# Moving a small transfer from SyncE's queue to GpSimd's, and a large store and its subtractions earlier on GpSimd

## The reference, cut to what matters

```python
x = x + jnp.tanh(g_xattn[0]) * _L0_xattn_ref(_layernorm(x, axis=-1), ctx_2048, ctx_2048)
x = x + jnp.tanh(g_ffn[0]) * _L0_ffn_ref(_layernorm(x, axis=-1), L0_ffn_wg, L0_ffn_W, L0_ffn_b)
# attention, x is (16, 128, 512): 8 heads of 16 features, 512 x 512 scores for each head
qk = jnp.einsum('bdm,bdn->bmn', qh, kh) * scale
sm = jax.nn.softmax(qk, axis=-1)
ret = jnp.einsum('bmn,bcn->bcm', sm, vh)
# feed-forward: each of 2048 tokens goes to the one of 8 experts with the largest logit
```

## Time and profile before

| | |
|---|---|
| median of 3 runs | 585.63 us (582.6 to 586.23) |
| the profiled execution: its time | 586.23 us |
| the profiled execution: its span | 584.6 us, from the first to the last instruction |
| busy shares of the span | PE 88%, DVE 72%, ACT 60%, POOL 60% |
| mean granted TensorE clock | 0.977 |

### The profile page before, as it was taken

One profiled execution on the slowest core, in us unless ns is written; L12 is line 12 of the kernel. 1 busy time (PEld: TensorE's weight loads), 2 busy tenths in 40 slices (PEclk: granted clock), 3 DMA queues, 4 the chain that ended last, 5 costly groups with the idle time before them and its releaser, 6 DMA issues. The chain is left out here.

```text
span 584.6 us, 9983 instructions
## 1 busy us (share of the span) xinstructions
PE 515.4 (88%) x2603; PEld 183.0 (31%) x2603; DVE 422.7 (72%) x831; ACT 349.7 (60%) x429; POOL 352.5 (60%) x568
## 2 busy tenths in 40 slices
PE   0389999889887999998999999998979979899994
PEld 0012323222323232323333232323322235355551
DVE  5898988768785789888999998989998565112121
ACT  3217887758684778786887877886855842111110
POOL 7444478756564657685767777885473446544532
PEclk9999999989997899999999999999997999999998
DMA  4875457666666486776557555545540154643410
GB/s 141 237 154 178 140 174 201 217 176 185 185 191 176 131 229 197 197 205 175 161 162 213 166 171 153 165 127 158 127 116 24 38 181 163 186 138 98 127 55 0
DMA packets 50392, 90.90 MB, mean 156 GB/s; under 512 B 22018, under 2 KB 24066, under 8 KB 50320
## 3 DMA queue, kind: packets, MB, share of 16 engines
q1 hardware_dynamic: 36096, 65.28, 40.9%
q0 software_dynamic: 10560, 24.93, 12.9%
q10 hardware_dynamic: 3696, 0.23, 0.4%
HBM read 66.91 MB, written 28.41 MB: 163 GB/s over the span
## 5 line engine op out<-in xcount | busy, mean ns | idle before, releaser
L948 DVE TENSOR_REDUCE neg_max<-ps_ring 128x1 f32<-128x512 f32 x480 | 309.0, 682 | 48.9 <-PE ps_ring L1315 47.6
L852 ACT ACTIVATE probs<-ps_scores 128x1024 f32<-128x1024 f32 x256 | 250.1, 1022 | 75.0 <-PE ps_scores L1334 74.2
L1315 PE MATMUL ps_ring<-stacks 96*128 96x512 bf16 x480 | 171.2, 393 | 14.8 <-DVE neg_max L948 13.7
L1334 PE MATMUL ps_scores<-stacks 128*128 128x512 bf16 x512 | 157.1, 390 | 14.9 <-DMA stacks<-shift_parts 8.5
L1357 PE MATMUL ps_pv<-probs,v_ones 128*32 128x512 f32 x992 | 135.2, 618 | 0.0
L1315 PEld LDWEIGHTS ps_ring<-stacks 96*128 96x128 bf16 x480 | 47.1, 98 | 171.4 <-DVE neg_max L948 125.1
L1420 PE MATMUL ps_scores<-w_sb,f_xt 128*128 x184 | 83.2, 593 | 0.0
L1334 PEld LDWEIGHTS ps_scores<-stacks 128*128 128x128 bf16 x512 | 48.2, 102 | 70.4 <-ACT probs L852 21.6
L836 ACT COPY f_xt<-ps_scores 128x512 f32<-128x512 f32 x23 | 13.5, 586 | 72.2 <-PE ps_scores L1401 72.2
L605 POOL CAST shift_parts<-shift 16x128 bf16<-16x128 f32 x32 | 9.0, 282 | 64.6 <-DVE shift L955 64.3
L1420 PEld LDWEIGHTS ps_scores<-w_sb,f_xt 128*128 128x128 f32 x184 | 34.5, 190 | 33.0 <-issue 32.2
(11 more groups left out here) (149 smaller groups left out, 499.8 us busy)
## 6 DMA issues: line engine op xcount, KB each, us to landing
stacks<-parts_dram SPq DMA_DIRECT2D x224, 64.0 KB, 3.0
parts_dram<-prep POOLq DMA_DIRECT2D x15, 768.0 KB, 5.4
w_sb<-w_t SPq DMA_DIRECT2D x16, 512.0 KB, 4.9
recs_dram<-rec SPq DMA_DIRECT2D x16, 512.0 KB, 3.2
stacks<-parts_dram SPq DMA_DIRECT2D x32, 192.0 KB, 3.4
prep<-x_perm SPq DMA_DIRECT2D x16, 256.0 KB, 2.9
prep<-k_perm SPq DMA_DIRECT2D x16, 256.0 KB, 3.2
v_in<-v_t SPq DMA_DIRECT2D x16, 256.0 KB, 3.3
```

The lines of the kernel that those rows point to most:

```text
L852: nc.scalar.activation(probs[:, k % 2, 2 * jp:2 * jp + 2], ps_scores[:, jp], ACT.Exp).then_inc(exp_done, 1)
L948: nc.vector.tensor_reduce(neg_max[:, g, j, c:c + 1], ps_ring[:, SLOT[tile]], AX.X, ALU.max, negate=True).then_inc(ring_free, 1)
L1315: nc.tensor.matmul(ps_ring[:, SLOT[tile]], q_stack[0:KS, into.p, g, j, c * 128:(c + 1) * 128], k_stack[0:KS, into.p, g, j], start=True, st ...
L1334: last = nc.tensor.matmul(ps_scores[:, jp, j % 2], k_stack[0:KA, B.p, g, j, c * 128:(c + 1) * 128], q_stack[0:KA, B.p, g, j], start=True, ...
```

## The change

The changed kernel does the following, and nothing else:

- SyncE has no `load_shift` any more. GpSimd issues group 0's three transfers too, and does so behind `rstd2(B-1)`, just before `copy_values(B+1)`; the one for batch 0 goes between `split_maxima(Batch(0, 0), 0)` and `rstd1(Batch(1, 0))`.
- On GpSimd `lows(B+3)`, with its 768 KB store, stands directly behind `rests(B+3)`, ahead of `add_high(B-1)`; it was behind `rstd2(B-1)`.
- On VectorE `invert_taken(B-1, 1)` goes from behind tile (2, 0) to behind (2, 2), `stats2(B-1)` from (5, 2) to (6, 0), `mean2(B-1)` from (5, 3) to (6, 1).

```diff
--- before.py
+++ after.py
@@ -405,15 +405,6 @@
                     at = 32 * j + g * DH
                     sp.dma_start(scale[at:at + DH, g], recip_dram[g, j].partition_broadcast(DH)).then_inc(recips_in[g], 16)
 
-            def load_shift(B, g):
-
-                sp.wait_ge(shift_ready, B.b * 2 + (g + 1))
-                if not isinstance(B.b, int):
-                    stand_alone(sp)
-                for t in range(NP):
-                    sp.dma_start(q_stack[KS + t:KS + t + 1, B.p, g].rearrange("o j (c m) -> o (j c) m", c=NC),
-                                 shift_parts[:, g, t]).then_inc(shift_in[g], 16)
-
             def load_weights(B):
 
                 n = NC * NE * DM // NB
@@ -449,8 +440,6 @@
             for g in range(NG):
                 load_stack(Batch(0, 1), g)
             load_values(Batch(0, 1))
-            sp.wait_ge(pads_in, 16)
-            load_shift(Batch(0, 0), 0)
             load_rows_keys(Batch(1, 1))
 
             def emit(B, prev, prev2, nxt, prep):
@@ -467,8 +456,6 @@
                     sp.wait_ge(dve_const, DVE_CONSTS)
                 if stack:
                     load_stack(B.plus(2), 0)
-                if not B.known(NB - 1):
-                    load_shift(B.plus(1), 0)
                 if not isinstance(B.b, int) or B.b + 4 < NB:
                     load_rows_keys(B.plus(4))
                 if by_transfer(B):
@@ -708,6 +695,7 @@
             rests(Batch(0, 1))
             lows(Batch(0, 1))
             split_maxima(Batch(0, 0), 0)
+            load_shift(Batch(0, 0), 0)
             rstd1(Batch(1, 0))
             rests(Batch(1, 0))
             lows(Batch(1, 0))
@@ -738,6 +726,7 @@
                     add_low(B.plus(-1))
                 if prep:
                     rests(B.plus(3))
+                    lows(B.plus(3))
                 if B.known(RANKED[1]):
                     number_places(1)
                     store_tokens(*GROUPS[1])
@@ -746,8 +735,7 @@
                 split_maxima(B.plus(1), 0)
                 if prev:
                     rstd2(B.plus(-1))
-                if prep:
-                    lows(B.plus(3))
+                load_shift(B.plus(1), 0)
                 copy_values(B.plus(1))
                 if B.known(RANKED[0]):
                     pool.wait_ge(table_set, 16)
@@ -1236,11 +1224,11 @@
                             mean1(B.plus(3))
                         if prev:
                             attended = B.plus(-1)
-                            if at == (2, 0):
+                            if at == (2, 2):
                                 invert_taken(attended, 1)
-                            if at == (5, 2):
+                            if at == (6, 0):
                                 stats2(attended)
-                            if at == (5, 3):
+                            if at == (6, 1):
                                 mean2(attended)
                         if by_transfer(B):
                             if at == (6, 2):
```

## The result

The changed kernel takes **608.21 us** (median of 4, 604.59 to 614.85) against 585.93 of the kernel before beside it: a ratio of 1.037, 95% interval 1.029 to 1.045. It is slower by 22 us; forecast were 11. One of the four executions (614.85) was in a slower state with a lower clock, and the ratio leaves it out. The profiled execution took 612.86 us, with a span of 611.2 (before: 586.2 and 584.6): some 4 us of the 26.6 between the two are this execution's own.

The account below looks back on a forecast made before the run. Batches 2 to 5 were taken as bound by SyncE's queue, 6 to 14 by PE. 586.2 + 8.7 for GpSimd's chain + 3 for the earlier store gave 597.9 profiled, 597 us as median; range 586 to 610.

Parts of the forecast that it names:

- rival C: Rival: early store delays the sums, batches 1 to 7 pass 29 us, shift lands 0.5 later afterwards; 611 us; chance 0.12.
- GpSimd's chain in batch 8: GpSimd's order summed from batch start: three shift issues begin at 22.8 us, landing at 26.4, where PE could start at 24.3.
- Batches 8 to 14: Attention stage's second half, held by the shift's landing: batch 8 +2.1 us, batches 9 to 13 +6.7, batch 14 +1.0.
- Batches 0 and 15 have one half of the chain or none: 0: First and last attention batches: GpSimd's longer order was taken to add nothing, 0 us.
- The batches of the first half: Batches 1 to 7: -1.1 us by the sum over GpSimd's order and +3 for the early store, +1.9 forecast.
- The congestion term: Batches 1 to 7: the earlier store competes with SyncE's loads and delays the sums; +3 us, bounds 0 to 10.
- C's mark: Sign of the congestion rival: VectorE's wait for the sums grows over 10 us in all.
- C's other half: Batches 8 to 14: the shift's own landing is 0.5 us longer, +3.5 in all.
- The landing in the loop: Batch 4's sum: issues start at 24.0 us, last one 1.0 later, 2.6 more to landing, giving 27.6.
- A: Rival: SyncE's relief brings batches 2 to 7 to about 26.5 us; needs first issue by 21.0; 576 us; chance 0.08.
- B's mechanism: Rival, even: the shift lands in 1.5 us instead of 2.6, each of 14 batches 1.1 shorter; 582 to 591; chance 0.22.
- The signs: Expected in the changed profile: longer PE shift waits, alike batches, no GpSimd idle before `add_high`, issues near 22.8, SyncE's loads earlier.

Follow-up runs that it names:

- e8_first: The changed kernel with batch 0's shift issued by SyncE again, with a semaphore of its own: 604.41 us, ratio 1.032 to the kernel before.
- e11_both: The changed kernel with group 0's shift directly behind `split_maxima`, ahead of `rstd2`, and batch 0's shift back on SyncE: 593.43 us, ratio 1.014 to the kernel before.
- e5_after_early: The changed kernel with group 0's shift moved directly behind `split_maxima`, ahead of `rstd2`: 596.55 us, ratio 1.019 to the kernel before.
- e7_fill: The changed kernel with eight extra matmuls on TensorE at each batch's start, ahead of the wait for the shift: 600.07 us, ratio 1.029 to the kernel before.
- e3_lows: The kernel before with only `lows` and its store moved ahead of `add_high`: 589.79 us, ratio 1.010.
- e10_sp: The change without its queue move: `lows` early and VectorE's new places, shift left on SyncE: 583.44 us, ratio 0.996 to the kernel before.
- e6_store: The changed kernel with the 768 KB store moved behind the shift's transfers, `lows`' subtractions staying early: 601.50 us, ratio 1.026 to the kernel before.
- e1_early: The kernel before with only group 0's shift moved to GpSimd, directly behind `split_maxima`, ahead of `rstd2`: 579.91 us, ratio 0.993.
- e2_late: The kernel before with only group 0's shift moved to GpSimd, behind `rstd2` with `lows` behind it: 593.34 us, ratio 1.016.

## Why the prediction was right, and where its size was off

The direction, the late shift behind GpSimd's chain and the range were right: 608 lies in 586 to 610. The size was not, and the range held partly by luck: 608 is outside the forecast's own 592 to 606 and nearer to rival C's 611, and is covered because half of C was taken in. Three quarters of the loss, 18.0 of the 24.3 us by batches, came in batches 0 to 7, where 1.9 was forecast. Point by point:

**GpSimd's chain in batch 8** was right to 0.2 us (23.0 against 22.8). The landing there was short: 1.6 us from the last of three issues, so 25.7 instead of 26.4. The prediction's picture of before has the same fault: the shift of batch 8 landed not at 24.5, just in time, but at 23.5. **Batches 8 to 14** together: +6.3 measured (1.4 + 6.4 - 1.5), +9.8 forecast (2.1 + 6.7 + 1.0). Batches 9 to 13 were +6.4 against +6.7; batch 14 got shorter, which was not foreseen.

**"Batches 0 and 15 have one half of the chain or none: 0"** was wrong by 3.5 us. Batch 0 has no chain at its end, but the three issues for its own shift stand ahead of the preparing of batch 2, and a SyncE issue there had cost GpSimd nothing. GpSimd's and ScalarE's rows of the changed kernel:

```profile
46.13 0.92 POOL L555 DMA_DIRECT2D parts_dram<-prep  x1 [0.30 <-POOL prep L553]
...
55.14 0.62 ACT L797 CAST prep<-prep 128x512 bf16<-128x512 f32 x1 [4.72 <-DMA parts_dram<-prep]
```

The store of batch 2 was issued at 44.05 before, 2.1 earlier. `cast_high` for batch 3 needs that store to have landed, since it writes where the store reads; ScalarE stands 4.72 us, and the scores behind it with it. With that shift back on SyncE (`e8_first`) the same cast is:

```profile
51.61 0.62 ACT L802 CAST prep<-prep 128x512 bf16<-128x512 f32 x1 [1.83 <-DMA parts_dram<-prep]
```

Batch 0 then takes 24.6 us, and in `e11_both` 25.9 after 30.6 in `e5_after_early`. In the six kernels in which GpSimd issues batch 0's shift, that batch takes 28.5 to 30.6 us, in the seven others 24.6 to 26.4. So the traces show this term and its cause, though the steps of 3.8 and 3.1 us in the times are within the noise.

**The batches of the first half** were mis-sized: batches 1 to 7 measured +14.5 (5.7 + 8.8), forecast +1.9 (-1.1 by the sum, +3 for the store). Three things stand in that gap.

- The clock, absent from the sum. TensorE stands before a batch (before batch 4, in the last step of batch 3), and part of the batch's first step then runs at a granted 0.5. TensorE's first step takes 3.85 us at full clock (310.98 to 314.83 in batch 9); in batches 3 to 7 it took 6.1, 4.9, 5.2, 5.3 and 6.0 in the trace (137.89 - 131.82 in batch 3), 27.5 together for 19.3: 8 us, and up to 1 more, since a batch's first matmul can be missing in the trace. Some of it was there before: batches 3 and 5 took 5.4 and 7.2, 4.8 more than 2 x 3.85. So the change adds 3 to 4 us by this in these batches. It is not only a loss of its own. VectorE's copy of the maxima of group 1, from which GpSimd's chain starts, came at 135.41 in batch 3, 4.0 after the start, and at 288.01 in batch 8, 2.7 after it; so 1.3 us of the dip pass into the next shift, which makes TensorE stand again. The prediction said that a late batch doesn't shorten the next; it should have said that a slow start lengthens it. `e7_fill` shows that dips come from the standing, but not what they cost by themselves.
- The congestion term. The wait for the sums grew from 6.5 to 14.4 us in this execution, over the 10 in all that the prediction set as C's mark if it meant the total, 2 under it if it meant the growth. Taken were +3, with 10 as the upper bound; the two long waits, in batches 1 and 3, are 10.4 us alone. That the early store makes them is not shown. One profiled execution each of the six other kernels with the store as early has 0 (`e3_lows`), 3.4 (`e7_fill`), 6.9, 8.3, 8.5 and 12.3 us (`e10_sp`, no slower than before); the kernels with the store late have 4.2 to 6.7. The store may take part; what decides whether the sums come late stays open. C's other half, a landing 0.5 longer in batches 8 to 14, did not come.
- The landing in the loop. The first issues began at 23.9 to 25.9 in batches 2 to 7 (forecast 24.0), but the last landed 4.1 to 5.1 us after the first was issued, and not 3.6. With the store behind them it was no better (3.8 to 5.4 us in batches 1 to 7 of `e6_store`, and 5.9 to 7.1 in batches 2 to 7 of `e1_early`), so the stack's loads are the likelier company; this was not tried alone. The kernel before had shown a long landing there: the rows below the list.

The first row is for SyncE's shifts of batches 2 to 7 in the kernel before, the second for those of batches 8 to 14:

```profile
DMA to landing us min/median/max: 2.8/3.6/4.5
...
DMA to landing us min/median/max: 1.7/2.1/3.0
```

The prediction took one median, GpSimd's 2.6, for both halves: 1.0 less than the first row's, 0.5 more than the second's.

These terms overlap (a late sum also makes TensorE stand), and the experiments' 3.8, 8.1, 6.7 and 11.7 us, of which only the last is clear of noise, add up to more than the loss; they aren't shares of it.

**The rivals.** A was wrong for this change but real: with the shift ahead of `rstd2` and `lows` behind, the first issue comes before 21 in most batches (22.5 in batch 2, 21.1 in batch 9) and the kernel gains (579.9, not the 576 worked out). B's mechanism, the short landing, held in the second half alone: 1.5 to 2.0 us from the last issue in batches 8 and 10 to 14, but 3.0 to 4.1 in batches 1 to 7.

**The signs.** TensorE's wait: 20 to 25 us in 12 or more, measured 26.7 in 12. Batches 26.4 to 27.6: near it in batches 8 to 13 (25.7 to 27.8), not in 1 to 7 (28.5 to 33.9). `add_high`'s idle time gone: yes. SyncE has the record and key loads right behind the stack's: yes, and nothing came of it, since in the changed kernel SyncE waits for VectorE's reciprocal instead (85.1 us in 22, before 20.0 in 11).

**What stays open.** `e11_both` is 10 us above `e10_sp` (593.4, 583.4); the two differ in who issues the shift from batch 1 on. TensorE's 13.1 us before `turn_rows`, absent in `e10_sp`, is enough to explain it, but no kernel took that wait away by itself, so a cost of its own of issuing from GpSimd is not excluded.

## What to carry to other kernels

An issue that is cheap on one engine's queue is not free on another's: write down what that engine owes at the end of each round (here the shift and `rstd2`) and put the transfer first only if nothing of the same due time stands behind it. The place in the order decided the sign, -0.7% ahead of `rstd2` and +1.6% behind it. Look at the prologue too when a step moves; and when a change makes TensorE stand at each round's start, add what the clock then costs. Take a transfer's landing time from rows of the stretch in which it will run, not from a median over all.

## What the runs showed of the hardware

**TensorE's clock after it stood.** Windows of the changed kernel around the starts of batches 3, 5 and 8, the end of one batch and the first step of the next:

```profile
127.79:131.82 4.03, 0.38 (x4) 0.27 (x4) 0.67 (x1) 0.94 (x2) 1.29 (x4) 0.82 0.50 130
131.82:138.00 6.18, 6.18 (x25) 2.40 (x25) 2.92 (x6) 2.73 (x3) 1.40 (x4) 0.57 0.32 89
192.00:194.60 2.60, 0.40 (x4) 0.18 (x4) 0.69 (x1) 0.58 (x1) 0.66 (x2) 1.00 0.35 113
194.60:200.00 5.40, 5.19 (x25) 2.13 (x27) 2.81 (x6) 2.73 (x3) 1.28 (x4) 0.68 0.35 99
282.54:285.30 2.76, 0.00 (x1) 0.01 (x1) 0.29 (x1) 0.58 (x1) 0.01 (x1) 1.00 0.37 117
285.30:289.36 4.06, 3.99 (x25) 1.98 (x27) 2.95 (x6) 2.63 (x3) 0.54 (x2) 1.00 0.33 80
```

TensorE worked 0.38 of 4.03 us, and 0.40 of 2.60, and the step behind had a granted clock of 0.57 and 0.68, a mean of the two levels 1.2 and 2.4 GHz. Standing doesn't always end so. Before batch 8 TensorE stood for the whole 2.76 us and the step ran at 1.00; in the kernel before, it stood 2.21 us before batch 3 and 2.16 before batch 4, and the steps behind ran at 0.68 and at 1.00. Before batch 9 it stood 0.89 us and no dip followed.

**A large store amid loads.** The 768 KB store, median of 15 from issue to landing, in the page of the kernel before and of the changed one, of the same form:

```profile
parts_dram<-prep POOLq DMA_DIRECT2D x15, 768.0 KB, 5.4
```

```profile
parts_dram<-prep POOLq DMA_DIRECT2D x15, 768.0 KB, 7.3
```

In the other kernels with the store early it is 6.4 (`e3_lows`) to 7.7 (`e11_both`), in `e1_early` and `e2_late`, with the store late, 4.6 and 4.8: going out among the loads costs it some 2 us.

**Small transfers of GpSimd** took 2.8 us in the median from issue to landing in the changed kernel, as SyncE's did before; the least were 1.5 and 1.7. The Trainium skill, DMA: Bandwidth & Descriptors, Specifications, has GpSimd's first byte 0.4 us later than SyncE's; between these two medians that doesn't show.
